# Four places for the second experts' scaled rows, half slots one full slot sooner, and the last two full slots' products interleaved

## The reference, cut to what matters

```python
def _L1_ffn_ref(x, Wg, W11, W12, W2):
    B, S, H, I, E, K = (2, 512, 256, 512, 8, 2)
    gate_scores = jax.nn.softmax(x @ Wg, axis=-1)
    topk_scores, topk_idx = jax.lax.top_k(gate_scores, K)
    topk_scores = topk_scores / (topk_scores.sum(-1, keepdims=True) + 1e-08)
    gate = jnp.einsum('bsh,ehi->bsei', x, W11)
    value = jnp.einsum('bsh,ehi->bsei', x, W12)
    fused = gate * jax.nn.sigmoid(gate) * value
    expert_out = jnp.einsum('bsei,eih->bseh', fused, W2)
    gathered = jnp.take_along_axis(expert_out, topk_idx[..., None], axis=2)
    out = jnp.sum(topk_scores[..., None] * gathered, axis=2)
    return out
x = x + _L1_ffn_ref(_layernorm(x, axis=-1), L1_ffn_Wg, L1_ffn_W11, L1_ffn_W12, L1_ffn_W2)
```

## Time and profile before

| what | value |
|---|---|
| time, median of 3 runs | 1079.97 us (1078.24 to 1096.52) |
| the profiled execution's own time | 1084.37 us |
| its span, first to last instruction | 1082.6 us |
| PE busy | 1013.5 us (94%), 7526 matmuls |
| DVE busy | 712.6 us (66%) |
| ACT busy | 660.2 us (61%) |
| POOL busy | 518.3 us (48%) |
| mean granted TensorE clock | 0.982 of full |
| mean rate of all transfers | 157 GB/s |

### The profile page before, as it was taken

The page is one execution under the profiler, slowest core; times in us unless marked ns, Lnnn a source line. Parts: engine busy times, 40 slices in busy tenths (PEclk is TensorE's granted clock), DMA queues, the critical chain, the costliest instruction groups (busy, mean ns, idle before and its releaser), DMA issues. The chain is left out here.

```text
span 1082.6 us, 24137 instructions
## 1 busy us (share of the span) xinstructions
PE 1013.5 (94%) x7526; PEld 941.8 (87%) x7526; DVE 712.6 (66%) x2216; ACT 660.2 (61%) x2446; POOL 518.3 (48%) x524
## 2 busy tenths in 40 slices
PE   7899998799999999889999999997999999998993
PEld 4688888699999999667999999896999999998993
DVE  5778886444554544567777877767767677666673
ACT  2699996444554553359999999864344444443441
POOL 2356776433332223326668887755532333323233
PEclk9999999799999999999999999999999999998997
DMA  9920001566666676400112222358797586874772
GB/s 314 345 87 21 31 31 52 203 230 223 224 214 225 214 255 219 142 16 30 40 45 75 75 70 70 123 154 252 216 280 208 126 234 174 252 223 81 230 234 34
DMA packets 95490, 169.71 MB, mean 157 GB/s; under 512 B 12322, under 2 KB 70308, under 8 KB 93860
## 3 DMA queue, kind: packets, MB, share of 16 engines
q1 hardware_dynamic: 79028, 142.33, 38.7%
q0 software_dynamic: 16368, 26.23, 11.2%
HBM read 150.67 MB, written 62.43 MB: 197 GB/s over the span
## 5 line engine op out<-in xcount | busy, mean ns | idle before, releaser
L802 ACT ACTIVATE L_prob<-psum,L_neg_max 128x64 f32<-128x64 f32 x768 | 229.3, 364 | 4.8 <-DVE L_neg_max L1128 4.7
L1730 PE MATMUL psum<-E_xT_hi,E_up_w 128*128 128x256 f32 x1024 | 189.8, 282 | 7.8 <-DVE E_xT_lo L1978 4.9
L802 ACT ACTIVATION_READ_ACCUMULATOR L_prob<-psum,L_neg_max 128x1 f32 x768 | 196.0, 258 | 0.0
L2141 POOL DMA_INDIRECT out<-E_y,E_dest x64 | 105.6, 1650 | 173.0 <-DMA out<-E_y,E_dest 90.2
L1730 PEld LDWEIGHTS psum<-E_xT_hi,E_up_w 128*128 128x128 f32 x1024 | 159.8, 189 | 10.6 <-issue 6.1
L1730 PE MATMUL psum<-E_xT_lo,E_up_w 128*128 128x256 f32 x512 | 143.5, 280 | 1.1 <-issue 1.1
L1884 ACT ACTIVATE E_sg<-psum 128x256 f32<-128x256 f32 x128 | 48.6, 383 | 111.3 <-PE psum L1730 106.8
L840 POOL TENSOR_TENSOR L_prob<-L_prob,L_rcp 128x512 f32<-128x512 f32 (+1 forms) x64 | 94.4, 1476 | 44.8 <-DVE L_rcp L1092 43.9
L747 PE MATMUL psum<-L_n_hi,L_pT_hi 128*128 128x256 f32 x384 | 108.1, 282 | 3.8 <-DVE L_pT_lo L1135 3.8
L1370 ACT ACTIVATE E_h_hi<-psum 128x256 fp32r<-128x256 f32 (+1 forms) x128 | 55.7, 438 | 85.8 <-PE psum L1312 85.8
L747 PE MATMUL psum<-L_n_lo,L_pT_hi 128*128 128x256 f32 x384 | 106.6, 278 | 0.0
(11 more groups left out here) (283 smaller groups left out, 3089.4 us busy)
## 6 DMA issues: line engine op xcount, KB each, us to landing
E_up_w<-up SPq DMA_DIRECT2D x26, 2048.0 KB
E_w<-in_w SPq DMA_DIRECT2D x16, 1024.0 KB, 7.2
E_w<-in_w SPq DMA_DIRECT2D x29, 512.0 KB
E_half_up_w<-up SPq DMA_DIRECT2D x28, 512.0 KB
E_xin<-rows SPq DMA_DIRECT2D x32, 260.0 KB
E_raw<-in_w SPq DMA_DIRECT2D x16, 512.0 KB, 6.7
up<-E_raw_hi SPq DMA_DIRECT2D x16, 512.0 KB, 6.2
up<-E_raw_lo SPq DMA_DIRECT2D x16, 512.0 KB, 3.7
```

Of the source, the lines that this page charges most:

```text
L802: last = e.activation(prob[q][:, h * KEYS:(h + 1) * KEYS], scores_ps(t)[:, h * KEYS:(h + 1) * KEYS], ACT.Exp, bias=nmx[:, q, h, :], accum_ ...
L1730: mm = q.matmul(bank, up_w[wpar(i, par)][:, half, w, c, m * P:(m + 1) * P], x[:, c, :], start=(k == 0), stop=(k == 3 * KC - 1))
L2141: q.indirect_dma_start(p.out[:, :], bass.IndirectOffsetOnAxis(ap=dest[:, par, c, :], axis=0), y[:, par, c, :], None, compute_op=ALU.add).t ...
```

## The change

1. `y` becomes four tensors and `wt` and `dest` get four places (index i mod 4). `place` of slot i now waits for the add of slot i - 4.
2. In each group the half slot's steps move one full slot ahead on every engine: its first product stands after slot a + 1, and its add between those of a + 1 and a + 2. Its load pieces move along on SP's queue. The loop has four rounds instead of five; group 5 and the last two full slots are straight code.
3. On PE, half slot 6 stands before slot 30's first product instead of before slot 31's, `down` of slot 30 goes between the second and third `up` of slot 31, and slot 31's own second product (`down_last`) does three quarters of its sums for both halves before it waits for the last quarter of the hidden values. DVE scales slot 30's result in the middle of slot 31.

```diff
-    y = at(124, "y", [P, 2, TC, D])
-    wt, dest = at(170.25, "wt", [P, 2, TC, 1]), at(170.5, "dest", [P, 2, TC, 1], I32)
+    y = [at(k, f"y{j}", [P, TC, D]) for j, k in enumerate((124, 126, 104, 106))]
+    wt, dest = at(170.25, "wt", [P, 4, TC, 1]), at(170.5, "dest", [P, 4, TC, 1], I32)
...
     def front(j):
-        return group(j) + (0 if is_int(j) and j == NH - 1 else 2)
+        return group(j) + (-1 if is_int(j) and j == NH - 1 else 1)
...
-        with eng.Fori(1, NH - 1) as j:
+        with eng.Fori(1, NH - 2) as j:
             body(j)
-        last(group(NH - 1))
+        last(group(NH - 2))
... (SP)
+        def half_rest(j, a):
+            e = entry(q, 1, NF + j, E - 1)
+            load(q, a + 1, 1)
+            half_x(q, j)
+            half_piece(q, j, e, 2)
+            load(q, a + 2, 0)
+            half_piece(q, j, e, 3)
+            half_w2(q, j, e)
+            load(q, a + 3, 1)
         def last(a):
             j = NH - 1
+            half_rest(j - 1, a)
             e = entry(q, 1, NF + j, E - 1)
+            half_piece(q, j, e, 0)
             half_piece(q, j, e, 1)
             half_x(q, j)
-            load(q, a + 1, 1)
+            load(q, a + 4, 0)
             half_piece(q, j, e, 2)
             half_piece(q, j, e, 3)
             half_w2(q, j, e)
+            load(q, a + 5, 1)
... (PE)
+    def down_last(q, i, par):
+        b = wpar(i, par)
+        wait(q, s_w2lo, splits(i))
+        for ms in (range(FC - 1), range(FC - 1, FC)):
+            wait(q, s_hlo, i * FC + ms[-1] + 1)
+            for c in range(TC):
+                if ms[0] == 0:
+                    wait(q, s_y, TC * i + c - 1)
+                for m in ms:
+                    for k, (a, w) in enumerate(((h_hi, w2_hi), (h_lo, w2_hi), (h_hi, w2_lo))):
+                        mm = q.matmul(ps[:, Y_BANK + c, 0:D], a[:, par, m, c * P:(c + 1) * P], w[:, b, m, :],
+                                      start=(m == 0 and k == 0), stop=(m == FC - 1 and k == 2))
+                if ms[-1] == FC - 1:
+                    mm.then_inc(s_dn, 1)
...
+        def around(j, a):
+            ups(a, 0)
+            transposes(q, a + 1, 1)
+            down(q, a - 1, 1)
+            ups(a + 1, 1)
+            half_transposes(q, j)
+            down(q, a, 0)
+            half_up(q, j)
+            transposes(q, a + 2, 0)
+            down(q, a + 1, 1)
+            half_turn(q, j)
+            ups(a + 2, 0, j)
+            transposes(q, a + 3, 1)
+            half_down(q, j)
+            ups(a + 3, 1)
         def body(j):
             a = group(j)
...
+            around(j, a)
             transposes(q, a + 4, 0)
-            half_down(q, j)
+            down(q, a + 2, 0, half=j)
         def last(a):
             j = NH - 1
-            ups(a, 0)
+            around(j - 1, a)
             half_transposes(q, j)
-            down(q, a - 1, 1, half=j - 1)
+            down(q, a + 2, 0, half=j - 1)
             half_up(q, j)
-            transposes(q, a + 1, 1)
-            down(q, a, 0)
+            transposes(q, a + 4, 0)
+            down(q, a + 3, 1)
             half_turn(q, j)
-            ups(a + 1, 1, j)
+            ups(a + 4, 0, j)
+            transposes(q, a + 5, 1)
             half_down(q, j)
-            down(q, a + 1, 1, half=j)
+            for m in range(FC):
+                if m == 2:
+                    down(q, a + 4, 0, half=j)
+                up(q, a + 5, 1, m)
+            down_last(q, a + 5, 1)
... (DVE)
-    def place(q, i, par):
+    def place(q, i, four):
         wait(q, s_mt, NM * (i + 1))
-        wait(q, s_add, 16 * TC * (i - 1))
-        q.tensor_copy(dest[:, par, :, :], mb[:, :, :])
+        wait(q, s_add, 16 * TC * (i - 3))
+        q.tensor_copy(dest[:, four, :, :], mb[:, :, :])
```

More of the change, by code:

```diff
@@ L1947, in body @@
             full(a, 0)
-            full(a + 1, 1)
-            full(a + 2, 0, j)
+            full(a + 1, 1, j)
             half(j)
+            full(a + 2, 0)
             full(a + 3, 1)
         def last(a):
-            full(a, 0, NH - 1)
+            full(a, 0)
+            full(a + 1, 1, NH - 2)
+            half(NH - 2)
+            full(a + 2, 0)
+            full(a + 3, 1, NH - 1)
             half(NH - 1)
-            full(a + 1, 1, last=True)
+            full(a + 4, 0)
+            full(a + 5, 1, last=True)
         slots(q, body, last)
@@ L2061, in vector, with full @@
     def vector(q, rest):
-        def full(i, par, half=None, behind=None, last=False):
-            small = meta(q, i, par)
+        def full(i, four, half=None, behind=None, last=False):
+            par = four % 2
+            small = meta(q, i, four)
             for m in range(FC):
+                if last and m == 2:
+                    outputs(q, i - 1, (four - 1) % 4)
                 hidden(q, i, m)
@@ L2083, in full @@
             assert small.j == NM
-            if behind is None:
-                outputs(q, i - 1, 1 - par)
-            else:
+            if behind is not None:
                 half_outputs(q, behind)
-            place(q, i, par)
+            elif not last:
+                outputs(q, i - 1, (four - 1) % 4)
+            place(q, i, four)
         def half(j):
@@ L2098, in half @@
             q.tensor_tensor(hw2_lo[:, :, :], hw2[:, :, :], hw2_hi[:, :, :].bitcast(F32), ALU.subtract).then_inc(sh_w2lo, 1)
[L2099 removed]
+            outputs(q, front(j), 1 if is_int(j) and j == NH - 1 else 3)
             q.wait_ge(sh_hhi, j + 1)
@@ L2113, in body @@
             a = group(j)
-            full(a, 0)
-            full(a + 1, 1)
-            full(a + 2, 0, half=j)
+            full(a, 2)
+            full(a + 1, 3, half=j)
             half(j)
-            full(a + 3, 1, behind=j)
+            full(a + 2, 0, behind=j)
+            full(a + 3, 1)
         def last(a):
-            full(a, 0, half=NH - 1)
+            full(a, 2)
+            full(a + 1, 3, half=NH - 2)
+            half(NH - 2)
+            full(a + 2, 0, behind=NH - 2)
+            full(a + 3, 1, half=NH - 1)
             half(NH - 1)
-            full(a + 1, 1, behind=NH - 1, last=True)
-            outputs(q, a + 1, 1)
+            full(a + 4, 2, behind=NH - 1)
+            full(a + 5, 3, last=True)
+            outputs(q, a + 5, 3)
         slots(q, body, last)
@@ L2132, in half_add, with add @@
                              hy[:, :], None, compute_op=ALU.add).then_inc(sh_add, 16)
-    def add(q, i, par, half=None):
+    def add(q, i, four, half=None):
         wait(q, s_add, 16 * TC * i)
@@ L2140, in add @@
             land(q, i)
-            q.indirect_dma_start(p.out[:, :], bass.IndirectOffsetOnAxis(ap=dest[:, par, c, :], axis=0),
-                                 y[:, par, c, :], None, compute_op=ALU.add).then_inc(s_add, 16)
+            q.indirect_dma_start(p.out[:, :], bass.IndirectOffsetOnAxis(ap=dest[:, four, c, :], axis=0),
+                                 y[four][:, c, :], None, compute_op=ALU.add).then_inc(s_add, 16)
     def gpsimd_end(q, t):
```

67 lines of the change are left out of this document (24 added, 43 removed).

## The result

The changed kernel takes 1092.89 us (median of 20 runs, 1084.26 to 1100.1), the kernel before 1082.66 (20 runs, 1076.62 to 1096.52). The ratio is 1.0091, with a 95% interval of 1.0066 to 1.0116: **slower by 0.9%, some 10 us**. The forecast was 1076, 4 us under the 1079.97 of the first three runs of the kernel before.

What follows compares the result with a forecast made beforehand. It took PE to bound the loop and the chain of adds the end. PE's 6.0 us gain counted only in part; add 31 starting 2.9 + 1.1 us earlier took the median 1079.97 to 1076 us, range 1069 to 1082.

Steps and rivals of the forecast that it cites:

- The step that failed: Half slot's steps one slot sooner in the loop: same distances from loads to use on PE, so cost 0.
- The size at half slot 6: New PE wait before half slot 6's first product, its pieces behind slot 30's loads: 0 to 3 us, taken as 1.
- The chain decides: At the end, add 31 starts 6 us after its data, so the chain of adds sets the time, not PE.
- the sum on the chain's side: Chain of adds up to add 31: it starts 2.9 and 1.1 us earlier, at 1067.6, making the span 4.0 us shorter.
- the first term: Four places: DVE's 6.19 us wait at the dest cast and PE's stop before half slot 4 go, PE 5.83 us earlier.
- the 5.83 us: Gain on PE from group 4 on, once its 2.98 us stop before half slot 4 and the low clock go.
- rival C's first half: Ordinary executions have a shorter dest wait and no PE stop, so nothing is gained: about 1079.5; whole rival's chance 0.10.
- The sign that I named for it: Median is 4.4 us under the profiled execution, close to the price of PE's stop before half slot 4.
- Half slot 5's 1.15 us: PE's wait for half slot 5's weights goes, as the piece moves from behind slot 29's loads to slot 28's: 1.15 us.
- The interleaving: Slot 30's down among slot 31's ups at the end: PE's sum the same within 0.5 us, taken as 0.
- gain on the chain: At the end, interleaving readies h6 and slot 30's rows sooner, leaving only add 31 after PE's end.
- B: Weights issued sooner slow the adds in groups 4 and 5, add 31 2.4 us later: 1082.4, chance 0.12.

Runs made afterwards that it cites:

- e6: Kernel before, with the full slot's load ahead of each half slot's last piece always fetched: 1094.15 us, 1.0155 of the kernel before.
- e1: Changed kernel, with each half slot's last two weight pieces issued ahead of the full slot's load: 1084.52 us, 1.0030 of the kernel before.
- e11: Changed kernel, with only the last half slot's pieces and second weights issued ahead of slot 30's load: 1090.09 us, 1.0060 of the kernel before.
- e5: Changed kernel, half slots' last two pieces and second weights ahead of the load, half slot 0's second piece behind slot 7's: 1071.77 us, 0.9950 of before.
- e9: e5 with the half slot's dest cast moved later, to just before its scaling: 1080.36 us, 0.9975 of the kernel before.
- e10: e5 with the end as the kernel before has it, not interleaved: 1080.85 us, 0.9943 of the kernel before.
- e7: Kernel before, old order, with four places and the half slot's last piece and second weights ahead of the load: 1072.76 us, 0.9985 of the kernel before.
- e2: Kernel before with only the four places for y, wt and dest, old order: 1083.47 us, 0.9993 of the kernel before.
- e12: The same kernel as e2, run again in another set: 1084.38 us, 0.9987 of the kernel before.
- e4: Changed kernel with the end as the kernel before has it, not interleaved: 1090.09 us, 1.0079 of the kernel before.
- e8: e5 with the old wait at the dest cast, for the add two slots back: 1079.12 us, 1.0026 of the kernel before.
- e3: Changed kernel with the old wait at the dest cast, for the add two slots back: 1091.46 us, 1.0074 of the kernel before.

## Why the prediction was wrong

**The step that failed** is "It is the same work in a turned order: the distances from its loads to their use on PE are the same in slots", with "In the loop I cost it at 0". The distances are the same in slots, but the loads that lie in them are not, because which loads fetch depends on the data. Shifting the half slot by one moved its last piece from behind slots 9, 13, ..., 29 to behind 8, 12, ..., 28 and 30. I looked at one of the seven, slot 30. In the loop the 0 measured 8.7 us (2.3 + 6.4). e6 shows that a fetched load ahead of the piece suffices for such waits; without it two thirds of the loss go in e1, about a third in e11, where only the last of the three is removed, and all of it in e5, which moves the second weights too. Each of the seven could have been read beforehand from the 0.33 and 0.08 us of SP's rows.

**The size at half slot 6.** I gave "0 to 3 us", took 1, and said it was hidden behind the adds. It was 3.58, and with the 2.5 us of half clock 6.1, and nothing hid it: the adds waited for their rows. The clock was missing from the term, although show the same price behind a wait of 2.98. From slot 30's first weights (1035.65) to the landing (1049.97) were 14.3 us for my 15. That is nearly right by luck: I divided by the 253 GB/s of a mean over 45 us, while the stretch itself ran at 332, with other transfers in it. And PE stood ready 10.8 us after that issue (1050.01 - 3.58), not 12.

**"The chain decides"** was false for the changed kernel, since PE's 15 us of new waits let the adds catch up (20 waits for data, 9 for landings). It is true of the profiles of e5 and e9, where these waits are gone: there the last adds follow each other without waiting for data, as the sum on the chain's side had it; in e10 add 30 waits for its rows. So the kernel that I described is nearer to e5 than to the change. That e5's 0.5%, 5 us, is near the 4 that I gave is in part luck: e5 moves loads that I did not have in the sum, and e7, in the old order, comes within 1 us of it.

**The four places** did what the first term says: the waits at the cast and the stop before half slot 4 are gone, and that group takes 40.32 us. But the 5.83 us were read from a single execution. e2 and e12 put the part at about 1 us in the old order, with 4 us inside both intervals. This is rival C's first half, which I had given 0.10. The sign that I named for it was weak: the profiled time stood 4.4 us over the median of three runs, but 1.7 over that of twenty.

**Half slot 5's 1.15 us** went as forecast: its piece now stands behind slot 28's load, which doesn't fetch. **The interleaving** at 0 on PE was right (1.31 us of waiting for the 1.4 forecast), and its "gain on the chain" isn't to be seen in e4 or e10.

**The rivals.** B said slower, by way of the adds in groups 4 and 5, and I held against it that "the same bytes move in the same order". The result has B's sign by another way: the same bytes, but in another order against those that need them. No case of mine had the half slots' weights late in the loop, so the range ended at 1082.

The Trainium skill, page "DMA: Bandwidth & Descriptors", section "Issuing engines are not separate DMA queues", says that transfers started by different engines share the same 16 DMA engines and interleave. From this I estimate that issuing the piece from another engine would give it a share of the rate at once instead of after the load, but take that from the load. The trace shows the 16 engines full in the three stretches (0.96 to 1.05); the other engine was not tried.

**Still open:** why the old wait costs more in the new order (e8), which the traces don't show, and where e5's gain over e1 comes from. Both the second weights and half slot 0's second piece moved; the second weights' wait of 1.85 us is gone, and with the granted clock of 0.66 in the 5 us behind it I estimate its cost at 3.6 us of the 8.6, while slot 7's wait stays (1.51 for 1.79).

## What to carry to other kernels

When a step is moved in a cyclic order, list for every transfer of it which transfers stand ahead in its queue in each round, before and after, and look in the trace at which of them really fetch: a conditional load may make an issue that is free in one position cost 2 to 6 us in the next. Put the piece that is needed soonest ahead of the large load that is needed a slot later; here this was worth 1.4% of the changed kernel. Where a reordering is judged, put the same loads right in the old order too: here that was as fast (e7). A single stop in one profiled execution is priced against the median before it is called a gain.

## What the runs showed of the hardware

- The length of a wait of PE doesn't alone tell what the clock does behind it. In the 5 us behind waits of 3.38 us (e6), 3.51, 3.58, 3.65 (e8) and 4.38 us (e5) the granted clock was 0.50 to 0.54. Behind shorter ones both occur: 0.66 behind 1.85 (e1) and 1.89 us (e2), 1.00 behind 2.32; 0.50 behind the 2.98 us of the kernel before (982 to 987), 0.66 behind 3.13 (e11), 1.00 behind 3.15 us (e6); and in e3, behind waits of 2.44, 2.61 and 2.92 us, in this order (stretches, columns as in the earlier trace rows):

```profile
904.00:909.00 5.00, 5.00 (x24) 4.42 (x25) 1.58 (x4) 1.66 (x2) 1.80 (x2) 0.66 0.69 109
948.50:953.50 5.00, 5.00 (x24) 4.37 (x25) 1.45 (x3) 1.66 (x2) 2.52 (x2) 0.66 0.75 151
1056.40:1061.40 5.00, 5.00 (x39) 4.68 (x39) 2.78 (x9) 1.63 (x2) 1.61 (x2) 1.00 0.23 49
```

  At 0.66 a stretch of 5 us loses 1.7 us, at 0.50 it loses 2.5. So where PE bounds, I estimate that a wait of 2.5 us costs 2.5 or 4 us, and one of 3.5 costs 6.
- At full clock the same 48 products of a slot's `ups` took 5.44 us in some slots and 5.66 in others, by their place in the group, and nothing in the profile tells why. Two links of the critical chain of after:

```profile
843.77 5.44 PE psum L1740 x48
...
858.68 5.66 PE psum L1740 x48
```
